# One statistics pass for Mamba's two norms, tanh in place of sigmoid, the first convolution tap on ScalarE, borrowed PSUM banks in the last expert layer, and a new order of turns

## What is computed

```
x = x + ssm(layernorm(x))        # in-projection, conv over 4 taps + silu on 1024 channels, decayed scan,
                                 # gate silu(z), LayerNorm, out-projection
x = x + ffn(layernorm(x))        # sigmoid(xr W_r) * (relu(xk W_k)^2 W_v)
x = x + mamba(layernorm(x))      # mamba(x): h = norm(x)*g + b; conv + silu; 16 states; returns x + out
x = x + experts_gelu(layernorm(x))     # 8 experts, top 2
x = x + attention(layernorm(x))        # linear attention, cumulative sums
x = x + ternary(layernorm(x))
x = x + scan(layernorm(x))       # x_in = silu(a) * sigmoid(b); A, B, C; scan; RMS norm; out-projection
x = x + experts_silu(layernorm(x))     # silu(gate) * up, 8 experts, top 2
```

## Time and profile before

| | |
|---|---|
| median of 3 runs | 1415.96 us (1413.04 to 1419.31) |
| profiled execution, first to last instruction | 1400.6 us |
| the profiled execution's own time | not given apart; the median of the runs lies 15.4 us above its span |
| TensorE matmul busy | 1104.8 us, 79% |
| VectorE busy | 890.9 us, 64% |
| ScalarE busy | 630.4 us, 45% |
| GpSimd busy | 281.7 us, 20% |
| HBM read and written | 91.24 MB and 14.75 MB |

### The profile page before, as it was taken

One profiled execution on the slowest core, in us unless ns is written; L12 is line 12 of the kernel. 1 busy time (PEld: TensorE's weight loads), 2 busy tenths in 40 slices (PEclk: granted clock), 3 DMA queues, 4 the chain that ended last, 5 costly groups with the idle time before them and its releaser, 6 DMA issues.

```text
span 1400.6 us, 15057 instructions
## 1 busy us (share of the span) xinstructions
PE 1104.8 (79%) x4959; PEld 698.7 (50%) x4959; DVE 890.9 (64%) x1919; ACT 630.4 (45%) x1194; POOL 281.7 (20%) x258
## 2 busy tenths in 40 slices
PE   4978657767977979686768676799999899897791
PEld 2536312334743634353457442574555556787781
DVE  6787879987558767767635789723735652363432
ACT  3433385424552348634237972273252434542330
POOL 3000113324120002130230244202000032014404
PEclk9999877777989999878889897999999999899996
DMA  8100000003520000000125420370000014468782
GB/s 322 47 0 1 0 0 0 0 1 118 163 61 1 0 0 1 0 0 0 45 92 177 131 74 21 96 224 21 1 1 0 1 63 132 157 214 283 260 277 69
DMA packets 49411, 107.02 MB, mean 76 GB/s; under 512 B 4840, under 2 KB 32368, under 8 KB 48688
## 3 DMA queue, kind: packets, MB, share of 16 engines
q1 hardware_dynamic: 44656, 92.74, 20.7%
q0 software_dynamic: 4096, 8.40, 2.0%
q10 hardware_dynamic: 576, 4.87, 0.8%
HBM read 91.24 MB, written 14.75 MB: 76 GB/s over the span
## 4 chain that ended last, share of the span: by engine, by line
PE 41%; DVE 22%; ACT 13%; issue 9%; POOL 7%; DMA 6%; SPq 1%; DVEq 0%; POOLq 0%; ACTq 0%
PE ps L1920 6%; PE ps L1638 5%; DMA expert_ring<-in_e_dram 4%; PE ps L1586 4%; PE ps L1752 4%; DVE up L1341 3%; PE ps L1858 3%; POOL slots_dram L717 3%; ACT big L957 2%; PE ps L1692 2%; PE ps L1829 2%; PE ps L1958 2%; DVE big L1348 2%; POOL up L727 2%; PE ps L1909 1%
## 5 line engine op out<-in xcount | busy, mean ns | idle before, releaser
L1858 PE MATMUL ps<-big,expert_ring 128*128 128x128 f32 x1160 | 158.0, 286 | 33.6 <-DMA expert_ring<-in_e_dram 20.4
L1858 PEld LDWEIGHTS ps<-big,expert_ring 128*128 128x128 f32 x1160 | 145.2, 199 | 48.0 <-DMA expert_ring<-in_e_dram 26.9
L1341 DVE TENSOR_TENSOR_SCAN up<-cv,big 128x512 f32<-128x512 f32 x128 | 152.5, 1230 | 21.5 <-ACT cv L908 17.4
L660 POOL TENSOR_TENSOR rstd<-ve,nhalf 128x4 f32<-128x4 f32 (+1 forms) x41 | 47.2, 1153 | 577.2 <-DVE ve L1119 470.6
L1752 PE MATMUL ps<-big,consts 128*128 128x512 f32 x256 | 154.3, 735 | 2.4 <-DVE big L1348 2.4
L697 POOL TENSOR_TENSOR big<-big,mt 128x512 f32<-128x512 f32 x64 | 85.8, 1344 | 279.1 <-ACT mt L901 152.6
L1920 PE MATMUL ps<-big,weights 128*128 128x512 f32 x256 | 115.4, 597 | 0.0
L1769 PE MATMUL ps<-q,row_pick 96*128 96x512 bf16 x128 | 54.5, 448 | 76.6 <-DVE big L1348 61.4
L1829 PE MATMUL ps<-expert_ring,big 128*128 128x128 f32 x792 | 107.6, 280 | 5.9 <-ACT big L957 3.6
L1829 PEld LDWEIGHTS ps<-expert_ring,big 128*128 128x128 f32 x792 | 98.9, 195 | 15.3 <-ACT big L957 9.8
L1459 DVE SCALAR_TENSOR_TENSOR big<-ps,expert_ring,key 128x128 f32<-128x128 f32 x184 | 51.8, 344 | 79.6 <-PE ps L1858 67.4
(11 more groups left out here) (247 smaller groups left out, 1943.4 us busy)
## 6 DMA issues: line engine op xcount, KB each, us to landing
expert_ring<-in_e_dram SPq DMA_DIRECT2D x46, 836.0 KB, 5.3
expert_ring<-in_e_dram SPq DMA_DIRECT2D x53, 578.0 KB, 4.4
big<-slots_dram SPq DMA_DIRECT2D x21, 256.0 KB, 3.5
results_dram<-mt SPq DMA_DIRECT2D x21, 256.0 KB, 5.3
weights<-in_w_dram ACTq DMA_DIRECT2D x1, 3072.0 KB, 15.5
slots_dram<-big SPq DMA_DIRECT2D x2, 1024.0 KB, 10.3
weights<-in_w_dram SPq DMA_DIRECT2D x1, 1600.0 KB, 8.6
x<-in_x_dram SPq DMA_DIRECT2D x4, 256.0 KB, 13.6
```

The lines of the kernel that those rows point to most:

```text
L1341: dve.tensor_tensor_scan(UP[s][:, j, PAD:PAD + T], CV[s][:, j, :], BIG2[s][:, j, :], 0.0, ALU.mult, ALU.add).then_inc(m_scan[s], 1)
L1858: last = pe.matmul(bank4(s, r if m else b % 2)[:, k, :], ring[:, q % RING, r * T + k * P:r * T + (k + 1) * P], XGT[s][:, b // 4 % 4, b % 4 ...
```

## The change

What it does:

- Mamba's statistics are taken once, of x. For the second norm the power is taken of v(1+e)+e*e, where v is the variance and e the epsilon, and both normalised sequences are made from x: first the twice-normalised one (`XH`, in `cv`), then the other (`XN`, in `key`), which is needed only at the layer's end.
- Each sigmoid(t) becomes tanh(t/2), and the 0.5(1+...) is taken into the operations behind it, into `s_abc` and `normw` (halved once) and into the scale of the RMS norm.
- The first tap and the bias of each convolution are a second ScalarE activation from PSUM (Identity with scale and bias), in ssm and in Mamba. VectorE keeps three taps. In the ssm layer this activation waits until the block two before it has been turned.
- In the last expert layer, stream 1 writes its odd blocks' gate and up products into stream 0's banks 0 and 1, after stream 0's last block; a gate or up matmul there waits for the block two before it in place of one before.
- All five tables in `RUNS` are new, and some turns are merged. Which layers of the two streams run beside each other stays the same to within a few turns.

The diff, with one line of the tables, and without the hunks that only drop or move a `yield` (some with the wait that stood beside it) or that pass the shorter argument list of `conv`:

```diff
@@ -138,44 +138,45 @@
-        1, 1, 1, 1, 1, 1, 12, 5, 2, 3, 2, 3, 1, 1, 3, 2, 1, 2, 2, 2, 2, 5, 3, 2, 2, 5, 27, 1, 3, 1, 4, 1, 4,
...
+        1, 2, 2, 1, 10, 2, 1, 1, 1, 1, 1, 3, 2, 3, 3, 1, 1, 2, 2, 1, 1, 3, 2, 3, 1, 1, 1, 1, 1, 2, 1, 4, 21,
...
@@ -534,6 +535,12 @@
+        def expert_bank(m, s, r, b):
+
+            if m and s % NS == 1 and b % 2:
+                return bank(s - 1, r)
+            return bank(s, r if m else b % 2)
+
         def chunk(s, c):
@@ -685,8 +692,11 @@
             def mamba(s):
-                yield from ln(n2o, s)
-                yield from ln(n2, s)
+                for n, at in ((n2, NC), (n2o, 0)):
+                    yield
+                    pool.wait_ge(n.var[s], n.var.at(s, 0))
+                    pool.tensor_tensor(rstd[s][:, at:at + NC], ve[s][:, at:at + NC], nhalf[:, 0:NC], ALU.pow)\
+                        .then_inc(n.rs[s], 1)
                 for n in range(NM):
@@ -796,7 +806,11 @@
                             act.wait_ge(l0_cv[s], l0_cv.at(s, b - 2))
-                        act.activation(UP[s][:, b % 2, PAD:PAD + T], bank(s, b % 2), ACT.Copy).then_inc(l0_up[s], 1)
+                        act.activation(UP[s][:, b % 2, PAD:PAD + T], bank(s, b % 2), ACT.Copy)
+                        if b >= 2:
+                            act.wait_ge(l0_xt[s], l0_xt.at(s, b - 2))
+                        act.activation(CV[s][:, b % 2, :], bank(s, b % 2), ACT.Identity, bias=pr("conv0_b", b),
+                                       scale=pr("conv0_w", 4 * b + 3)).then_inc(l0_up[s], 1)
                     if b >= 1:
@@ -864,14 +878,16 @@
                 act.wait_ge(f0_p[s], f0_p.at(s, 1))
-                act.activation(BIG1[s][:, 6, :], bank(s, 1), ACT.Sigmoid).then_inc(f0_sg[s], 1)
+                act.activation(BIG1[s][:, 6, :], bank(s, 1), ACT.Tanh, scale=0.5).then_inc(f0_sg[s], 1)
...
                     act.wait_ge(m_uz[s], m_uz.at(s, j))
-                    act.activation(UP[s][:, j, PAD:PAD + T], bank(s, j), ACT.Copy).then_inc(m_up[s], 1)
+                    act.activation(UP[s][:, j, PAD:PAD + T], bank(s, j), ACT.Copy)
+                    act.activation(CV[s][:, j, :], bank(s, j), ACT.Identity, bias=pr("conv1_b", j),
+                                   scale=pr("conv1_w", 4 * j + 3)).then_inc(m_up[s], 1)
                 for j in range(2):
@@ -951,10 +967,10 @@
                             if m:
-                                last = act.activation(SG[s][:, b % 2, cols], bank(s, 0)[:, cols], ACT.Silu,
+                                last = act.activation(SG[s][:, b % 2, cols], expert_bank(m, s, 0, b)[:, cols], ACT.Silu,
                                                       bias=bias[:, k:k + 1])
                             else:
-                                last = act.activation(HID[s][:, b % 4, cols], bank(s, b % 2)[:, cols], ACT.Gelu,
+                                last = act.activation(HID[s][:, b % 4, cols], expert_bank(m, s, 0, b)[:, cols], ACT.Gelu,
                                                       bias=bias[:, k:k + 1])
@@ -1000,7 +1016,8 @@
                     act.wait_ge(s_ab[s], s_ab.at(s, 2 + j))
-                    act.activation(UP[s][:, j, PAD:PAD + T], bank(s, 2 + j), ACT.Sigmoid).then_inc(s_slg[s], 1)
+                    act.activation(UP[s][:, j, PAD:PAD + T], bank(s, 2 + j), ACT.Tanh, scale=0.5)\
+                        .then_inc(s_slg[s], 1)
                 yield
@@ -1153,10 +1170,9 @@
-            def conv(s, j, wcol, bcol):
+            def conv(s, j, wcol):
...
                 u, v = UP[s], CV[s]
-                step(dve.tensor_scalar(v[:, j, :], u[:, j, PAD:PAD + T], pr(*wcol(3)), pr(*bcol), ALU.mult, ALU.add))
                 step(dve.scalar_tensor_tensor(v[:, j, :], u[:, j, 2:2 + T], pr(*wcol(2)), v[:, j, :], ALU.mult, ALU.add))
@@ -1297,20 +1311,34 @@
                 dve.wait_ge(f0_sg[s], f0_sg.at(s, 0))
-                step(dve.tensor_tensor(b[:, 7, :], bank(s, 2), b[:, 6, :], ALU.mult))
-                add_x(s, b[:, 7, :].rearrange("p (c n) -> p c n", c=NC), x_done[1])
+                step(dve.scalar_tensor_tensor(b[:, 7, :], b[:, 6, :], 1.0, bank(s, 2), ALU.add, ALU.mult))
+                dve.scalar_tensor_tensor(X[s][:, :, :], b[:, 7, :].rearrange("p (c n) -> p c n", c=NC), 0.5, X[s][:, :, :],
+                                         ALU.mult, ALU.add).then_inc(x_done[1][s], 1)
...
                 dve.wait_ge(x_done[1][s], x_done[1].at(s, 0))
-                yield from norm(n2o, s, (X[s], XN[s]))
-                yield
-                dve.wait_ge(n2o.done[s], n2o.done.at(s, 0))
-                yield from norm(n2, s, (XN[s], XH[s]))
+                for c in range(NC):
+                    last = dve.bn_stats(stat[s][:, c, 0, :], X[s][:, c, :])
+                step(last)
+                for c in range(NC):
+                    last = dve.bn_aggr(mv[s][:, c, :], stat[s][:, c, 0, :])
+                step(last)
+
+                dve.tensor_scalar(ve[s][:, NC:2 * NC], mv[s][:, 0:NC, 1], 1.0 + LN_EPS, LN_EPS * LN_EPS, ALU.mult,
+                                  ALU.add).then_inc(n2.var[s], 1)
+                dve.tensor_scalar(ve[s][:, 0:NC], mv[s][:, 0:NC, 1], LN_EPS, None, ALU.add).then_inc(n2o.var[s], 1)
+                for n, at, dst in ((n2, NC, XH[s]), (n2o, 0, XN[s])):
+                    yield
+                    dve.wait_ge(n.rs[s], n.rs.at(s, 0))
+                    for c in range(NC):
+                        last = dve.tensor_scalar(dst[:, c, :], X[s][:, c, :], mv[s][:, c, 0:1],
+                                                 rstd[s][:, at + c:at + c + 1], ALU.subtract, ALU.mult)
+                    last.then_inc(n.done[s], 1)
                 for j in range(2):
...
                     dve.wait_ge(m_up[s], m_up.at(s, j))
-                    conv(s, j, lambda t: ("conv1_w", 4 * j + t), ("conv1_b", j)).then_inc(m_cv[s], 1)
+                    conv(s, j, lambda t: ("conv1_w", 4 * j + t)).then_inc(m_cv[s], 1)
                 yield
@@ -1354,6 +1382,7 @@
                         .then_inc(m_mix[s], 1)
+                dve.wait_ge(n2o.done[s], n2o.done.at(s, 0))
                 add_x(s, XN[s][:, :, :])
@@ -1456,7 +1485,8 @@
                         cols = slice(k * P, (k + 1) * P)
-                        last = dve.scalar_tensor_tensor(HID[s][:, b % 4, cols], bank(s, 1)[:, cols], bias[:, k:k + 1],
+                        last = dve.scalar_tensor_tensor(HID[s][:, b % 4, cols], expert_bank(1, s, 1, b)[:, cols],
+                                                        bias[:, k:k + 1],
                                                         SG[s][:, b % 2, cols], ALU.add, ALU.mult)
@@ -1501,6 +1531,10 @@
                 add_x(s, bank4(s, 0), x_done[4])
+                if s == 0:
+                    dve.wait_ge(wsem[3], 16)
+                    dve.tensor_scalar(w("s_abc"), w("s_abc"), 0.5, None, ALU.mult)
+                    dve.tensor_scalar(pr("normw", 0, 2), pr("normw", 0, 2), 0.5, None, ALU.mult)
@@ -1520,8 +1554,8 @@
                     dve.wait_ge(s_slg[s], s_slg.at(s, 2 + j))
-                    dve.tensor_tensor(BIG1[s][:, j, :], CV[s][:, j, :], UP[s][:, j, PAD:PAD + T], ALU.mult)\
-                        .then_inc(s_xi[s], 1)
+                    dve.scalar_tensor_tensor(BIG1[s][:, j, :], UP[s][:, j, PAD:PAD + T], 1.0, CV[s][:, j, :],
+                                             ALU.add, ALU.mult).then_inc(s_xi[s], 1)
                 yield
@@ -1548,7 +1582,7 @@
                 dve.wait_ge(s_o[s], s_o.at(s, 0))
-                dve.tensor_scalar(ve[s][:, 0:NC], bank(s, 3)[:, 0:NC], 1.0 / 256, RMS_EPS, ALU.mult, ALU.add)\
+                dve.tensor_scalar(ve[s][:, 0:NC], bank(s, 3)[:, 0:NC], 1.0 / 1024, RMS_EPS, ALU.mult, ALU.add)\
                     .then_inc(s_var[s], 1)
@@ -1850,12 +1879,13 @@
                                     pe.wait_ge(g.gt[s], g.gt.at(s, b // 4))
-                                if m and b:
-                                    pe.wait_ge(g.act[s], g.act.at(s, b - 1))
-                            elif b:
-                                pe.wait_ge(g.h[s], g.h.at(s, b - 1))
+                            free = g.h if r else g.act
+                            if m and s % NS == 1 and b == 1:
+                                pe.wait_ge(g.h[s - 1], g.h.at(s - 1, NBLK - 1))
+                            elif m and b > s % NS:
+                                pe.wait_ge(free[s], free.at(s, b - 1 - s % NS))
                             for k in range(4):
-                                last = pe.matmul(bank4(s, r if m else b % 2)[:, k, :],
+                                last = pe.matmul(expert_bank(m, s, r, b)[:, k * P:(k + 1) * P],
                                                  ring[:, q % RING, r * T + k * P:r * T + (k + 1) * P],
```

More of the change, by code:

```diff
@@ L1661, in turn_block @@
                 def turn_block(s, j):
-                    yield
-                    if j >= 2:
-                        pe.wait_ge(l0_yn[s], l0_yn.at(s, j - 2))
```

(9 more changed lines are left out.)

25 lines of the change are left out of this document (10 added, 15 removed), and 60 rows, old and new, of the table RUNS.

## The result

| | median | lowest to highest | runs |
|---|---|---|---|
| kernel before | 1418.34 us | 1413.01 to 1424.77 | 10 |
| changed kernel | 1427.68 us | 1423.99 to 1433.29 | 10 |

A forecast was written before the change was run, and what follows sets the result against it. No engine was full overall (TensorE 79%, VectorE 64%, ScalarE 45%); the bounding engine changed by stretch. Terms 9.9 + 3.5 + 6.4 + 3.2 = 23.0 us took 1416.0 to 1393.0 us, 8-in-10 range 1368 to 1413.

The forecast's parts named there:

- New tables: New instruction order in all engines: taken at 0, bounded by 8 us either way beyond the other terms.
- One set of statistics: Norms ahead of Mamba: wanted sequence ready 4.12 and 3.77 us earlier in stream 0; term 9.9 us, bounds 4.1 to 15.8.
- The two norms have nothing beside them that would wait longer: Argument against the idle-time rival, about the two norms whose sequence was forecast 4.12 and 3.77 us earlier.
- First tap: First ssm, tap moved to ScalarE: 16 blocks gain 0.22 us each; term 3.5 us, bounds 0 and 8.1.
- Tanh: Ffn and scans: 23 fewer ScalarE table loads, mostly where ScalarE isn't waited for; term 6.4 us, bounds 0 to 15.
- The 72 loads: Sign expected in the changed kernel's profile: 72 ScalarE table loads, with ScalarE's busy time about the same.
- Borrowed banks: Stream 1's expert blocks: removes TensorE's wait for VectorE's product, not the ring's; term 3.2 us, bounds 0 to 12.3.
- The sum: Whole kernel: terms 9.9 + 3.5 + 6.4 + 3.2 = 23.0 us, taken from the 1416.0 median to give 1393.0 us.
- gains fall into idle time: Rival, whole kernel: only one norm (4.1) and two loads (2.6) stay, 6.7 us, giving 1409; chance 0.15.
- The slower rival: Tap's 24 new waits in ScalarE's queue cost 38.8 us against 23.0 gained, giving 1432 us; chance 0.10.
- The reference: Profiled span 1400.6 us, median 15.4 us above it; terms taken from the median of 1416.0 as they are.

## Why the prediction was wrong

- **New tables, taken at 0, bounded by 8 us: the step that failed and made a loss of the gain.** They cost 14.9 us (1429.09 against 1414.17). I had compared only which layers run side by side. Inside them the order decides three things that I didn't look at. Stream 0's first ffn ends 6.8 us later; TensorE waits there 1.7 us for a normalisation on VectorE (second row, from the second trace of the changed kernel), 0.8 in the old order (first). VectorE starts that normalisation at 127.66 in this trace, for 123.40 in the old order, and behind an addition to x (L1291) that stood after it there. TensorE's group starts 4.3 us later for it, which is most of the delay at that point (6.0 us by the ffn's end in this trace); no run tested it alone. In the first Mamba VectorE's scans fall beside GpSimd's multiplications. And the edits' worth depends on it: 14 us for tap, tanh and banks in this order, between two sessions.

```profile
124.27 3.15 PE L1699 MATMUL ps<-consts,big 128*128 128x128 f32 x19 [0.82 <-DVE big L1279]
```

```profile
128.53 5.08 PE L1702 MATMUL ps<-consts,big 128*128 128x128 f32 x24 [1.69 <-DVE big L1282]
```

- **One set of statistics, 9.9 us: measured 1.3** (below 4.3 by the interval). The norm did come 4.05 us earlier, as worked out from the earlier trace rows. "The two norms have nothing beside them that would wait longer" was false: TensorE's turn belonged to stream 1's ffn until 158.0. I had read VectorE's order there and not TensorE's.
- **First tap, 3.5 us: measured 3.4 to 4** in the old order (0.997 and 0.9966 against 0.9994, from other sessions and with overlapping intervals, so not told from nothing), and if it is there, not from where I took it. A block gains 0.58 us and not 0.22, in few blocks, and the layer doesn't end earlier.
- **Tanh, 6.4 us: measured 0.6** (below 4.1 by the interval). The 72 loads that I read off the new order are there, but with the old tables tanh removes only 12 of 95 and not 23: the new order with the sigmoids has 84, so 11 of the saved loads belonged to the order. In stream 1's last scan VectorE still waits, 5.0 us for 3.8 in the earlier trace rows:

```profile
DVE big L1557 <- ACT up L1019: 5.0, 1, 5.0
```

- **Borrowed banks, 3.2 us: measured 3.0 and 3.1.** That agrees with the term, though neither measurement by itself is told from nothing. In the new order TensorE waits 5.6 us for VectorE's product ahead of these matmuls with the old banks and at most 0.4 with the borrowed ones; the wait for the ring stays, and 5.4 us are idle with no wait that the profile shows, as in the stops:

```profile
L1888 PE MATMUL ps<-big,expert_ring 128*128 128x128 f32 x359 | 50.2, 293 | 12.0 <-DMA expert_ring<-in_e_dram 6.2 <-issue 5.4
```

- **The sum.** All edits in the old order gain 4.3 to 4.8 us, less than their single values added (8.3 to 8.9); they overlap, or it is within the intervals. That is the "gains fall into idle time" rival, 6.7 us, to which I gave 0.15. The new order then took 14.9. By the medians of the session that has all three kernels, forecast and measurement lie 33.7 us apart: 18.8 are the edits' terms, 14.9 the tables. So even without the tables the forecast of 23 us would have failed, on what an edit's freed time is worth.
- **The slower rival came near the time (1432) by a mechanism that isn't there.** TensorE's wait for the silu behind the new tap fell, from 27.5 us, and taking the tap back costs time:

```profile
PE ps L1662 <- ACT cv L827: 21.3, 17, 2.5
```

- **The reference.** The 15.4 us between the span and the median weren't overhead but the stops: in the runs that have both numbers the time is 1.8 to 3.1 us above the span. Taking the terms from the median kept the sum clear of that.

## What to carry to other kernels

When an edit makes something ready earlier on one engine, read in the next engine's own order what stands ahead of the consumer, before counting a gain. A new static order is a change of its own: run the edits in the old order first. Here that gives the fastest version that computes everything, 0.9966, and shows a loss that the edits hid: the tables cost 14.9 us, of which the total shows 9 to 11.

## What the hardware showed that I had not expected

**VectorE and GpSimd hold each other up.** The scan at 187.76 starts while GpSimd's multiplication (187.28 to 188.55) has 0.79 us to go, and takes 0.65 us more than the 1.21 us that is the mean with little work on GpSimd. The other way round GpSimd is held: its 32 multiplications take 1427 ns on average in the old order and 1357 in the new. So the same meeting costs the full engine in one order and the idle one in the other. The Trainium skill (SBUF — State Buffer, Who interferes with whom) says that a VectorE instruction with two SBUF inputs contends with a GpSimd instruction that reads SBUF. It calls the ports that the two share an exclusive lock, where the order of issue decides who blocks. The traces agree: the scan above runs over by most of the 0.79 us that the multiplication has left, and where the multiplication starts second, it is the one that takes longer, 2.04 us for 1.27 at 218.8. The forecast should have asked which scans the new order puts beside multiplications.

**Stops in the tail.** In four sessions of six ScalarE stands for 9 to 17 us twice, and VectorE and TensorE stop with it for part of that, beside 16 scatters and 16 gathers, whatever the kernel; this makes the tail some 20 us longer. The first line below is the page of the changed kernel, the second that of the kernel with little work for GpSimd, in a session without stops:

```profile
expert_ring<-in_e_dram SPq DMA_DIRECT2D x46, 836.0 KB
```

```profile
expert_ring<-in_e_dram SPq DMA_DIRECT2D x46, 836.0 KB, 4.8
```

All traces with stops lack the landing times of these loads, and all without have them. Whether the recording causes the stops or suffers from the same thing isn't known: no run tried it. The five later sessions also ran on five different chips, three with stops and two without, so the chip may be the cause as well.
